# A graph-attention layer on one core: VectorE scales the accumulator in place and adds to it, TensorE sums only two slots

## The reference

```python
q = (h @ Wq.T + bq).reshape(N, HEAD_DIM, HEADS) * scaling
k = (h @ Wk.T + bk).reshape(N, HEAD_DIM, HEADS)
v = (h @ Wv.T + bv).reshape(N, HEAD_DIM, HEADS)
s = jnp.einsum('edh,edh->eh', q[row], k[col])
m = jax.ops.segment_max(s, row, num_segments=N)
e = jnp.exp(s - m[row])
z = jax.ops.segment_sum(e, row, num_segments=N)
attn = e / z[row]
out = jax.ops.segment_sum(attn[:, None, :] * v[col], row, num_segments=N)
return out.reshape(N, -1) @ Wo.T + bo
...
x = _layernorm(x + _L0_gnn_ref(...))
```

## Time and profile before

| what | value |
|---|---|
| median of 3 runs | 4304.79 us |
| fastest and slowest of them | 4303.62 and 4323.05 us |
| span of the profiled execution | 4998.2 us |
| the profiled execution's own time beside the span | not recorded |
| TensorE (PE) busy | 4506.0 us |
| VectorE (DVE) busy | 2920.3 us |
| ScalarE (ACT) busy | 1624.4 us |
| GpSimd (POOL) busy | 2933.3 us |
| moved by DMA | 665.86 MB, 133 GB/s on average |

### The profile page before, as it was taken

How to read it: one execution, slowest core, us unless ns; L and a number is a source line. 1 busy time by engine, 2 the same in 40 slices (tenths; PEclk the granted TensorE clock), 3 DMA queues, 4 the chain that set the end, 5 groups by cost and what they waited for, 6 DMA issues and landing times. The chain is left out here.

```text
span 4998.2 us, 63175 instructions
## 1 busy us (share of the span) xinstructions
PE 4506.0 (90%) x8305; PEld 2637.9 (53%) x8305; DVE 2920.3 (58%) x7566; ACT 1624.4 (32%) x7078; POOL 2933.3 (59%) x2365
## 2 busy tenths in 40 slices
PE   4999999977810299999999999999999999999998
PEld 4567774333300155555555555555555555554565
DVE  6541454345461366666666666666666666666666
ACT  0100000111100144444444444444444444444322
POOL 2221120000076688888888888888888888886465
DMA  0100011111252366666666666666666666689222
GB/s 27 51 30 26 30 34 55 53 45 43 47 157 73 94 189 187 190 189 189 190 189 189 189 190 189 189 190 188 189 190 189 190 189 190 189 184 178 75 80 74
DMA packets 329217, 665.86 MB, mean 133 GB/s; under 512 B 63462, under 2 KB 191750, under 8 KB 329016
## 3 DMA queue, kind: packets, MB, share of 16 engines
q0 software_dynamic: 160768, 518.27, 38.1%
q1 hardware_dynamic: 168392, 146.96, 10.3%
HBM read 599.35 MB, written 65.86 MB: 133 GB/s over the span
## 5 line engine op out<-in xcount | busy, mean ns | idle before, releaser
L915 POOL DMA_INDIRECT kv<-kv_rows,idx x1794 | 2362.2, 1317 | 587.3 <-issue 560.8
L1025 PE MATMUL sum_ps<-pv,ident 128*128 128x264 f32 x2392 | 1612.1, 852 | 151.9 <-issue 146.7
L1025 PEld LDWEIGHTS sum_ps<-pv,ident 128*128 128x128 f32 x2392 | 847.4, 356 | 776.7 <-issue 606.5
L971 ACT ACTIVATE pv<-kv,s 128x33 f32<-128x33 f32 x4784 | 1081.1, 314 | 1.4 <-issue 1.4
L1029 PE MATMUL sum_ps<-pv,ident 128*128 128x264 f32 x1196 | 879.7, 857 | 0.1
L1027 PE MATMUL sum_ps<-pv,ident 128*128 128x264 f32 x1196 | 876.8, 854 | 1.9 <-issue 1.9
L833 DVE TENSOR_TENSOR pv<-acc,s 128x264 f32<-128x264 f32 x598 | 260.3, 435 | 876.1 <-ACT acc L980 782.5
L980 ACT ACTIVATE acc<-sum_ps 128x264 f32 x598 | 234.2, 392 | 1517.9 <-PE sum_ps L1029 1467.4
L797 DVE TENSOR_REDUCE s<-prod 128x24 f32<-128x768 f32 x598 | 569.9, 953 | 75.2 <-ACT pv L971 0.6
L1029 PEld LDWEIGHTS sum_ps<-pv,ident 128*128 128x128 f32 x1196 | 434.7, 364 | 300.9 <-issue 299.9
L790 DVE TENSOR_TENSOR prod<-kv,q 128x768 f32<-128x768 f32 x598 | 567.8, 950 | 42.9 <-DMA kv<-kv_rows,idx 41.4
(11 more groups left out here) (166 smaller groups left out, 3035.6 us busy)
## 6 DMA issues: line engine op xcount, KB each, us to landing
q<-q_perm SPq DMA_DIRECT2D x598, 128.0 KB
kv<-kv_rows,idx POOLq DMA_INDIRECT x1794
kv_rows<-kv_st SPq DMA_DIRECT2D x98, 260.0 KB, 2.3
xt_sb<-in_xT SPq DMA_DIRECT2D x98, 128.0 KB, 2.5
node_rows<-q_st SPq DMA_DIRECT2D x98, 128.0 KB, 2.6
q_perm<-kv_st SPq DMA_DIRECT2D x98, 128.0 KB
kv_st<-node_rows,node_id POOLq DMA_INDIRECT x98
cols<-edge_keys,run_at POOLq DMA_INDIRECT x98
```

The costliest lines, as they stand in the source:

```text
L915: pool.indirect_dma_start(out=kv[:, j, g, :], out_offset=None, in_=kv_rows, in_offset=bass.IndirectOffsetOnAxis(ap=idx[:, j, g:g + 1], axi ...
L971: last = act.activation(pv[:, b, V * VW + at_h:V * VW + at_h + HD + 1], kv[:, j, V, D + at_h:D + at_h + HD + 1], ACT.Copy, scale=s[:, b, V ...
L1025: pe.matmul(sum_ps[b][:, 0:VW], ident[:, :], pv[:, b, g * VW:(g + 1) * VW], start=g == 0, stop=False)
```

## The change

VectorE no longer writes the scaled accumulator to a fourth slot: it scales the accumulator in place (`scale_acc`, now behind `score` in the order), one pass later adds ScalarE's slot to it (`add_last`), and then adds TensorE's sum out of PSUM (`add_sum`). TensorE sums only the two slots that VectorE weighed. ScalarE's store is gone; its third slot waits for `add_last` in place of TensorE's sum. VectorE keeps three tile registers in place of two, since it still adds for step k - 1 when step k + 2 is looked up. TensorE's first six steps are written out ahead of its loop. `pv` has three slots in place of four, so the scratch row `tile_f` of the planning lies in a `kv` buffer.

```diff
-        pv = sb("pv", [P, 2, (G + 1) * VW])
+        pv = sb("pv", [P, 2, G * VW])
...
-        step_f, past, tile_f = room[:, 0:STEPS], room[:, STEPS:2 * STEPS], room[0:1, 2 * STEPS:3 * STEPS]
+        step_f, past, tile_f = room[:, 0:STEPS], room[:, STEPS:2 * STEPS], kv[0:1, U - 1, :, :].rearrange("p g w -> p (g w)")[:, 0:STEPS]
...
-                def carry(k, b, tile, first=False):
+                def scale_acc(k, b, tile, first=False):
+
                     if not first:
-                        dve.wait_ge(acc_stored, k)
-                    dve.tensor_tensor(pv[:, b, G * VW:].rearrange("p (h w) -> p h w", w=HD + 1),
-                                      acc[:, bass.ds(tile * VW, VW)].rearrange("p (h w) -> p h w", w=HD + 1),
-                                      s[:, b, G * HEADS:].unsqueeze(2).to_broadcast([P, HEADS, HD + 1]), ALU.mult).then_inc(carry_made, 1)
+                        dve.wait_ge(acc_added, k)
+                    dve.wait_ge(exp_made, k + 1)
+                    at_tile = acc[:, bass.ds(tile * VW, VW)].rearrange("p (h w) -> p h w", w=HD + 1)
+                    dve.tensor_tensor(at_tile, at_tile,
+                                      s[:, b, G * HEADS:].unsqueeze(2).to_broadcast([P, HEADS, HD + 1]), ALU.mult).then_inc(acc_scaled, 1)
+
+                def add_last(k, b, tile):
+
+                    dve.wait_ge(acc_scaled, k + 1)
+                    dve.wait_ge(last_made, k + 1)
+                    at_tile = acc[:, bass.ds(tile * VW, VW)]
+                    dve.tensor_tensor(at_tile, at_tile, pv[:, b, V * VW:G * VW], ALU.add).then_inc(last_added, 1)
+
+                def add_sum(k, b, tile):
+
+                    dve.wait_ge(last_added, k + 1)
+                    dve.wait_ge(summed, k + 1)
+                    at_tile = acc[:, bass.ds(tile * VW, VW)]
+                    dve.tensor_tensor(at_tile, at_tile, sum_ps[b][:, 0:VW], ALU.add).then_inc(acc_added, 1)
...
-                tile_r = [dve.alloc_register(f"tile_{b}") for b in range(2)]
-                col_r = [dve.alloc_register(f"col_{b}") for b in range(2)]
+                tile_r = [dve.alloc_register(f"tile_{b}") for b in range(3)]
+                col_r = [dve.alloc_register(f"col_{b}") for b in range(3)]
...
-                    look_up(k + 2, b)
+                    before = None if peel and j == 0 else bounded(dve, tile_r[(j + 2) % 3], TILES)
+                    look_up(k + 2, (j + 2) % 3)
+                    if before is not None:
+                        add_last(k - 1, b1, before)
                     mask_scores(k + 1, b1, col1, tile1)
-                    carry(k, b, tile, first=peel and j == 0)
                     maxima(k + 1, b1, tile1)
+                    if before is not None:
+                        add_sum(k - 1, b1, before)
                     if not last:
                         score(k + 2, (j + 2) % U, turn + (j + 2) // U)
+                    scale_acc(k, b, tile, first=peel and j == 0)
                     differences(k + 1, b1, tile1)
...
-                carry(k, k % 2, bounded(dve, tile_r[k % 2], TILES))
+                tile, before = bounded(dve, tile_r[k % 3], TILES), bounded(dve, tile_r[(k - 1) % 3], TILES)
+                add_last(k - 1, (k - 1) % 2, before)
+                add_sum(k - 1, (k - 1) % 2, before)
+                scale_acc(k, k % 2, tile)
+                add_last(k, k % 2, tile)
+                add_sum(k, k % 2, tile)
...
                     if not peeled:
-                        act.wait_ge(summed, k - 1)
+                        act.wait_ge(last_added, k - 1)
...
-                def store(k, b):
-
-                    v = act.value_load(step_tab[0:1, bass.ds(k, 1)], min_val=0, max_val=TAB * C * P - 1)
-                    tile = bounded(act, v & (P - 1), TILES)
-                    act.wait_ge(summed, k + 1)
-                    act.activation(acc[:, bass.ds(tile * VW, VW)], sum_ps[b][:, 0:VW], ACT.Copy).then_inc(acc_stored, 1)
...
                     weights(k + 1, (k + 1) % 2)
-                    store(k, k % 2)
...
-                def total(k, b):
+                def total(k, b, peeled=False):
 
                     pe.wait_ge(pv_made, k + 1)
+                    if not peeled:
+                        pe.wait_ge(acc_added, k - 1)
                     for g in range(V):
-                        pe.matmul(sum_ps[b][:, 0:VW], ident[:, :], pv[:, b, g * VW:(g + 1) * VW], start=g == 0, stop=False)
-                    pe.wait_ge(carry_made, k + 1)
-                    pe.matmul(sum_ps[b][:, 0:VW], ident[:, :], pv[:, b, G * VW:], start=False, stop=False)
-                    pe.wait_ge(last_made, k + 1)
-                    pe.matmul(sum_ps[b][:, 0:VW], ident[:, :], pv[:, b, V * VW:G * VW], start=False, stop=True).then_inc(summed, 1)
-
-                with pe.Fori(0, LOOPS) as kk:
+                        last = pe.matmul(sum_ps[b][:, 0:VW], ident[:, :], pv[:, b, g * VW:(g + 1) * VW], start=g == 0, stop=g == V - 1)
+                    last.then_inc(summed, 1)
+
+                for j in range(B):
+                    total(j, j % 2, peeled=j < 2)
+                with pe.Fori(1, LOOPS) as kk:
```

More of the change, by code:

```diff
@@ L713, in one_round @@
             sem(x) for x in ("prod_made", "scored", "old_copied", "masked", "max_made", "diffs_made"))
-        exp_made, pv_made, last_made, carry_made, summed, acc_stored = (
-            sem(x) for x in ("exp_made", "pv_made", "last_made", "carry_made", "summed", "acc_stored"))
+        exp_made, pv_made, last_made, acc_scaled, last_added, summed, acc_added = (
+            sem(x) for x in ("exp_made", "pv_made", "last_made", "acc_scaled", "last_added", "summed", "acc_added"))
         CUT = 512
@@ L837, in _, with look_up @@
                 dve.wait_ge(tab_ready, 1)
                 dve.wait_ge(runs_ready, 1)
-                tile_r = [dve.alloc_register(f"tile_{b}") for b in range(2)]
-                col_r = [dve.alloc_register(f"col_{b}") for b in range(2)]
-                def look_up(k, b):
+                tile_r = [dve.alloc_register(f"tile_{b}") for b in range(3)]
+                col_r = [dve.alloc_register(f"col_{b}") for b in range(3)]
+                def look_up(k, c):
                     v = dve.value_load(step_tab[0:1, bass.ds(k, 1)], min_val=0, max_val=TAB * C * P - 1)
-                    dve.reg_mov(tile_r[b], v & (P - 1))
-                    dve.reg_mov(col_r[b], v >> PBITS)
+                    dve.reg_mov(tile_r[c], v & (P - 1))
+                    dve.reg_mov(col_r[c], v >> PBITS)
@@ L852, in step @@
                     weigh(k, j % U, b, peeled=peel and j < 2)
-                    tile, tile1, col1 = bounded(dve, tile_r[b], TILES), bounded(dve, tile_r[b1], TILES), bounded(dve, col_r[b1], TAB * C - G)
-                    look_up(k + 2, b)
+                    tile, tile1, col1 = (bounded(dve, tile_r[j % 3], TILES), bounded(dve, tile_r[(j + 1) % 3], TILES),
+                                         bounded(dve, col_r[(j + 1) % 3], TAB * C - G))
+                    before = None if peel and j == 0 else bounded(dve, tile_r[(j + 2) % 3], TILES)
+                    look_up(k + 2, (j + 2) % 3)
+                    if before is not None:
+                        add_last(k - 1, b1, before)
                     mask_scores(k + 1, b1, col1, tile1)
-                    carry(k, b, tile, first=peel and j == 0)
                     maxima(k + 1, b1, tile1)
+                    if before is not None:
+                        add_sum(k - 1, b1, before)
                     if not last:
                         score(k + 2, (j + 2) % U, turn + (j + 2) // U)
+                    scale_acc(k, b, tile, first=peel and j == 0)
                     differences(k + 1, b1, tile1)
@@ L997, in _ @@
                         weights(k + 1, (j + 1) % 2)
-                        store(k, j % 2)
                         weigh_last(k + 1, (j + 1) % U, kk * (B // U) + (j + 1) // U, (j + 1) % 2)
@@ L1003, in _ @@
                     weights(k + 1, (k + 1) % 2)
-                    store(k, k % 2)
                     weigh_last(k + 1, (k + 1) % U, (k + 1) // U, (k + 1) % 2)
-                store(STEPS - 1, (STEPS - 1) % 2)
             @block.tensor
```

## The result

The kernel after takes 4142.9 us (median of 4 runs) against 4308.7 us; the ratio is 0.9635, with a 95% interval of 0.9593 to 0.9677. It is faster, and 4155 us had been forecast.

The account below looks back on a forecast made before the run. TensorE was taken to bound the profiled loop, with the gathers nearly as tight. A timed step was to fall from 4.50 to 4.25 us over 598 steps, 150 us off 4305, giving 4155 us; range 4000 to 4430.

Parts of the forecast that it names:

- What bounds the kernel before: Edge loop: TensorE sets the profiled step of 4.91 us, gathers nearly as tight at 4.85; timed step taken as 4.50.
- gathers hold both: Rival: the timed step is already the gathers' pace, so removing TensorE's work moves nothing; 4305 us, chance 0.17.
- TensorE's part: Sums in the loop: four of eight instructions go, 2.44 us a step; the remaining 2.5 us are covered by 5.1.
- ScalarE's part: ScalarE in the loop: loses the 392 ns store and its wait; it had slack, so nothing was counted.
- VectorE's part: VectorE's queue: a 1.49 us hole goes, two additions cost 0.70; 4.20 us a step, ends 3.94 and 4.49.
- GpSimd's part: Three gathers a step: 3.90 us free plus 0.35 of collisions, where 0.95 fell; step 4.25, ends 3.90 and 4.85.
- room to start freely: Gathers: 0.95 us of line 797 and the PSUM addition, neither with two SBUF operands, let gathers start unheld.
- The Trainium skill's lock: GpSimd can't write descriptors while VectorE holds their shared port pair, and goes on about 115 ns after release.
- that rival: VectorE's queue becomes the bound at 4.35 us a step, against 4.15 before: 120 us slower, 4425 us; chance 0.19.
- The clock did fall: Rival: half-idle TensorE gets a lower clock, its four instructions double to a 5.0 us step; 4605 us, chance 0.03.
- the 5.1 of cover: Time between the weighting and VectorE's addition of TensorE's sum one step later: 5.1 us, covering 2.5 us of TensorE work.

Follow-up runs that it names:

- the second profile: The kernel before, unchanged, profiled once more: time 4311.8 us, span 4310.1 us.
- two fillers: The kernel before with two added VectorE reductions a step, some 0.46 us each, one operand, read by nothing: 4065.6 us, ratio 0.9429.
- three slots on TensorE: The kernel after with ScalarE's slot summed by TensorE (six instructions) and no add_last: 4046.0 us, measured again 4015.3 us, ratio 0.9313.

## Why the prediction was right in its number and wrong in its reason

**What bounds the kernel before.** Wrong for the timed runs. "TensorE sets the step in this execution" was so in the profile of the earlier trace rows, where an instruction took 0.61 us; in the second profile four take 1.27 us in the step shown, and six instead of eight change nothing. I had seen that TensorE must be quicker when timed, and bounded the step at 4.15 to 4.85 us by it; the middle, 4.50, is near the 4.55 measured, but nothing spoke for the middle: that was luck. And I still let the change act on TensorE. The rival "gathers hold both" had the state of before right (the step is the gathers' pace), and its consequence, no change, wrong: it took that pace for a fixed one.

**TensorE's part.** "4 x 0.61 = 2.44 us of a step, on the path" is worth nothing when timed. That the sum is ready in time held: no wait for it worth a row.

**ScalarE's part.** Counted at nothing. No run took the store alone out or in, but two bear on it: two fillers, with the store left in, gave more than the change did, and the kernel without work on the accumulator, which has no store either, takes as long as before.

**VectorE's part.** Forecast 4.20 us between 3.94 and 4.49; measured 4.26. The additions took 419 and 433 ns each, as the rows said; the gap ahead of line 812 was 50.2 us in 376 steps, 0.13 us, where 0.11 of room had been left. The 0.18 us of register work ahead of line 844 was the miss: I took it to hide under line 825.

**GpSimd's part.** "I take 0.35" us of holds: 3 x 0.116 = 0.35 measured. But this is no term of its own: it is VectorE's 4.26 us less 3.90, and the 4.20 forecast for VectorE would have left 0.30, so the last 0.05 was luck. The reason given, room to start freely, is what the timeline shows for two of three gathers. What I did not see is that the holds depend on whether VectorE waits for kv, and so that VectorE's added work is not the price of the change but what brings its gain.

**The Trainium skill's lock** (SBUF — State Buffer, the section on a bandwidth-pool intuition) is told there of operations in a 2-port mode; for the operations on two operands here it is borne out as a lock too: a held gather ends 0.87 us after the operation that held it, so it loses the rest of that operation less 0.13 us. Its 115 ns between release and resumption can't be read from these rows, and setting them beside the 0.12 us by which 0.88 is less than an undisturbed gather, as I did, compared two different things. The same page (who interferes with whom) has it that reductions never contend, and the gather that started inside the filler, 1.00 us, agrees. By the rule alone the added operation on two operands would be lost time; but the kernel after, with more work on VectorE, has shorter holds than before (0.35 against 0.64 us a step), since what counts is where a gather starts.

**Rivals.** VectorE is the bound after, as that rival said, but at 4.26 and against 4.55 us. The clock did fall, to 0.50 of full speed in the loop. "The granted clock is 1.00 in every stretch" was a wrong reading: the first trace holds no record of the clock at all, and 1.00 there stands for none; the second profile of before has 0.78. The lower clock cost nothing, as four instructions at that clock end within 2.1 us, under the 5.1 of cover; the doubling to 5.0 us that I had priced was twice a time of the earlier trace rows, at 0.61 us an instruction. The warning of the Trainium skill (TensorE: Matmul & The Clock Gate, HAM oscillation), that the clock falls where TensorE idles, fits the fall, though no run tells whether it came about as that page has it, and none shows a loss by it.

## What to carry to other kernels

A profile whose span is 16% over the timed runs is not the loop that is timed: take a second profile before arguing from it. In a loop paced by gathers on GpSimd, work on VectorE isn't free or costly by its length alone: here, operations on two SBUF operands held a gather that started in them, and a VectorE that outruns the gathers ends up waiting for the very gather that it holds. Then filling VectorE a little past the gathers' free pace, here 3.9 us, is worth more than emptying it; the best version, three slots on TensorE and two operations on the accumulator, sits there at 4.05 us a step.

## What the runs showed of the hardware

The same program ran TensorE at 0.61 us an instruction through the loop of one profiled execution and at 0.3 to 0.5 us in another, whose granted clock in the loop was 0.78 on average. The trace of the first holds no record of the clock, so it can't say whether the clock explains the pace; an instruction took longer there than the 0.53 us at a granted clock of 0.50 in the kernel after. Why it was so slow stays open.

An operation on two SBUF operands and a gather shut each other out. Of 6767 gathers that started with over 0.14 us of such an operation (lines 790, 825, 833, 836, 844 or their counterparts) still to run, between 2000 and 3600 us of the fourteen traces, all but 114 ended 0.85 to 0.89 us after it. Those 114 had started within 0.05 us of the operation's own start. They took their free 1.00 us, and the operation was the longer one: a product took 1.01 us in the median in place of 0.95.

Useless reductions on one operand made a kernel 5.7% faster, and moving idle time away made another 3.8% slower. The threshold of 3.9 us is argued from rows and borne out by the kernels on either side of it (3.89 and 3.97 us of VectorE's queue); it was not tried with a gather path of another speed.
